# Attention: which engine copies which half of the transposed probabilities, and how the reciprocals of the row sums are spread

## The chip, the cores and the metric

The kernel runs on one core of a Trainium2 chip, in one launch. The metric is the device time of the launch in microseconds (us); lower is better. Engines: PE is TensorE (matmuls; PEld are its weight loads), DVE is VectorE, ACT is ScalarE, POOL is GpSimd, SP is SyncE, which issues most DMAs.

## The reference, cut to what matters

Two layers over x (2 x 512 x 1024) and a context (2 x 1024 x 1024): cross attention, a feed-forward block, a quantised product and a stream mixer. The change lies in the cross attention of the first layer:

```
query = q @ w_q.T; key = k @ w_k.T; value = v @ w_v.T     # 32 heads of 32; 8 groups of keys and values, 4 heads each
scores = einsum('bghnd,bgsd->bghns', query, key) / D_HEAD ** 0.5
scores = where(mask, scores, finfo.min)
attention = softmax(scores, axis=-1)
out = einsum('bghns,bgsd->bghnd', attention, value)
```

There are 2 x 8 = 16 pairs of batch and group; each has 512 queries (4 tiles of 128), 4 heads and 1024 keys (8 tiles of 128).

## The kernel before, in words

Stage a makes the queries, keys and values, stage b (line 452) is the attention, stages c, d and e are the rest. The stages follow one another; stage b ends with a barrier of all engines, and stage c starts after it, with some of its weights loaded early.

Stage b works in steps. One step is one tile of 128 queries of one head: 16 steps (`STEPS`) for a pair of batch and group, 256 steps in all. A loop body of 32 steps (two pairs, u = 0 and 1) stands first, 6 times in a hardware loop, and last. Each engine has its own list of instructions, written out by hand; semaphores order them. In step k (with j = k mod 16):

- TensorE (`body`, line 603) issues the scores of step k+2 (`score`, two matmuls of 512 keys into one of two PSUM buffers), then for the two halves f of the keys the four transposes of the probabilities `Pr` of step k into `psT` (line 621; the first half is called T1 below, the second T2), and between T1 and T2 the weighing of one tile of keys (`weigh`, line 575: four heads side by side, each 32 columns of the array, two records each). The weighing runs 8 steps behind: 8 steps (a unit: 4 heads x 2 query tiles) are collected in `PT`, and while the next 8 are transposed, one of 8 key tiles is weighed in each step.
- VectorE (`body`, line 729) masks the scores of step k+2 and takes their minimum (`mask_min`, line 700, one custom operation from PSUM to `Sc`), then copies the second half of the transposes of step k from `psT` to `PT` (`keep`, line 711).
- ScalarE (`body`, line 675) takes the exponential of step k+1 with the sum of each row (`exponentials`, line 647), then copies the first half of step k (`keep`, line 658).

What holds what: T1 and T2 of step k each wait until the copy of the same half of step k-1 is done, and T1 waits for the exponential of step k; the scores of step k+2 wait for the mask of step k; the mask waits for its scores; the exponential waits for its mask, and, with two `Pr` buffers, for T2 of two steps before.

The softmax is divided at the end. Each row is a query, but the output is held turned (head dimension by query), so the reciprocals of the 16 row sums of each query tile have to be spread over the partitions. For the pair that has just ended: VectorE takes the reciprocals (`reciprocals`, line 718, at j = 0), ScalarE copies the unscaled output (`keep_O`, line 669, j = 8), TensorE turns the reciprocals into 4 rows (`turn_rec`, line 590, j = 10, after T2), ScalarE copies these (`rec_rows`, line 665, j = 12), TensorE multiplies them by a constant 0/1 matrix `headsel` that gives each head its 32 partitions (`spread_rec`, line 599, j = 13, after T2), and VectorE multiplies (`normalise`, line 722, j = 15). SyncE stores the product and loads the next pair (line 546). GpSimd builds `ident` and `headsel` once.

Of the kernel before, what the change touches and what calls it, by code (L numbers as in the profile page):

```python
# [30 lines left out]
P = 128  # L31
# [420 lines left out]
def stage_b(nc, mask, QHd, QLd, KHd, KLd, Vd, AOd, early, start_early_loads):  # L452
# [4 lines left out]
    with ExitStack() as stack:  # L457
# [8 lines left out]
        UNIT = 2 * HPG  # L466
        UQ = 2 * P
        assert UNIT == NK
        ident = sb("b_ident", [P, P])
        headsel = sb("b_headsel", [HPG, P])  # L470
        mk8 = sb("b_mk8", [P, QT, S2], U8)
        mbias = sb("b_mbias", [P, QT, S2], BF16)
        Qs = sb("b_Qs", [P, 2, HPG, S], F32R)
        Ks = sb("b_Ks", [P, 2, S2], F32R)
        Vs = sb("b_Vs", [P, 2, NK, DH])
        Sc = sb("b_Sc", [P, 4, S2])
        Pr = sb("b_Pr", [P, 2, S2])
        PT = sb("b_PT", [P, 2, NK, HPG, UQ])
        mins = sb("b_mins", [P, 4])
        sums = sb("b_sums", [P, 2, STEPS])  # L480
        rec = sb("b_rec", [P, 2, STEPS])
        recT = sb("b_recT", [HPG, S])
        Os = sb("b_Os", [P, S])
        AOs = sb("b_AOs", [P, 2, S])
        psS = stack.enter_context(nc.psum_tensor("b_psS", [P, 2, S2], F32))
        psT = stack.enter_context(nc.psum_tensor("b_psT", [P, 2, NK // 2, P], F32))

        psO = stack.enter_context(nc.psum_tensor("b_psO", [P, 2, S], F32))

        setup = sem("b_setup")  # L490
        selready = sem("b_selready")
        mask_in = sem("b_mask_in")
        mbias_ready = sem("b_mbias")
        waited = sem("b_waited")
# [7 lines left out]
        kept = [sem(f"b_kept{f}") for f in range(2)]  # L502
        weighed = sem("b_weighed")
        rec_ready = sem("b_rec")
        rec_turned = sem("b_recturned")
        recT_ready = sem("b_recT")
        spread = sem("b_spread")
        O_kept = sem("b_Okept")
        AO_ready = sem("b_AO")
# [52 lines left out]
        @block.tensor  # L562
        def _(pe):
            def score(it, k, very_first=False):

                u, j = divmod(k, STEPS)
                qt, h = divmod(j, HPG)
                if j == 0 and not very_first:
                    pe.wait_ge(qkv_in[u], (it + 1) * (16 * QKV_DMAS))
                for n in range(2):  # L570
                    last = pe.matmul(psS[:, k % 2, n * HALF:(n + 1) * HALF], Qs[:, u, h, qt * P:(qt + 1) * P],  # L571
                                     Ks[:, u, n * HALF:(n + 1) * HALF], start=True, stop=True)
                last.then_inc(scored, 1)

            def weigh(it, k, first=False):

                u, unit, kt = (k // UNIT - 1) // 2 % 2, k // UNIT - 1, k % UNIT
                if kt == 0:
                    pe.wait_ge(kept[0], it * BODY + k)
                    pe.wait_ge(kept[1], it * BODY + k)  # L580
                    if unit % 2 == 0 and not first:
                        pe.wait_ge(AO_ready, it * 2 + (u - 1))
                cols = slice(unit % 2 * UQ, (unit % 2 + 1) * UQ)
                for h in range(HPG):
                    last = pe.matmul(psO[h * DH:(h + 1) * DH, u, cols], Vs[:, u, kt, :], PT[:, unit % 2, kt, h, :],  # L585
                                     start=(kt == 0), stop=(kt == NK - 1))
                if kt == NK - 1:
                    last.then_inc(weighed, 1)

            def turn_rec(bg, u):  # L590

                pe.wait_ge(rec_ready, bg + 1)
                pe.wait_ge(O_kept, bg + 1)
                for qt in range(QT):
                    last = pe.transpose(psO[0:HPG, u, qt * P:(qt + 1) * P], rec[:, u, qt * HPG:(qt + 1) * HPG],
                                        ident[:])
                last.then_inc(rec_turned, 1)

            def spread_rec(bg, u):
                pe.wait_ge(recT_ready, bg + 1)  # L600
                pe.matmul(psO[:, u, :], headsel[:], recT[:], start=True, stop=True).then_inc(spread, 1)

            def body(it, first=False, last=False):
                for k in range(BODY):
                    u, j = divmod(k, STEPS)

                    if not (last and k + 2 >= BODY):
                        pe.wait_ge(masked, it * BODY + (k + 1))
                        if k + 2 < BODY:
                            score(it, k + 2)  # L610
                        else:
                            score(it + 1, k + 2 - BODY)
                    pe.wait_ge(probs, it * BODY + (k + 1))
                    for f in range(2):
                        if f == 1 and not (first and k < UNIT):
                            weigh(it, k, first)
                        if not (first and k == 0):
                            pe.wait_ge(kept[f], it * BODY + k)
                        for t in range(NK // 2):
                            kt = f * (NK // 2) + t  # L620
                            last_t = pe.transpose(psT[:, f, t, :], Pr[:, k % 2, kt * P:(kt + 1) * P], ident[:])  # L621
                        last_t.then_inc(turned[f], 1)

                    if not (first and u == 0):
                        if j == UNIT + 2:
                            turn_rec(it * 2 + (u - 1), 1 - u)
                        if j == UNIT + 5:
                            spread_rec(it * 2 + (u - 1), 1 - u)

            pe.wait_ge(setup, 2)  # L630
            pe.wait_ge(selready, 4)
            pe.wait_ge(first_in, 16 * 8)
            score(0, 0, very_first=True)
            pe.wait_ge(qkv_in[0], 16 * QKV_DMAS)
            score(0, 1)
            body(0, first=True)
            with pe.Fori(1, BG // 2 - 1) as it:
                body(it)
            body(BG // 2 - 1, last=True)
            for k in range(UNIT):  # L640
                weigh(BG // 2, k)
            turn_rec(BG - 1, 1)
            spread_rec(BG - 1, 1)

        @block.scalar
        def _(act):
            def exponentials(it, k, first=False):

                act.wait_ge(masked, it * BODY + (k + 1))
                if not (first and k < 2):  # L650
                    act.wait_ge(turned[1], it * BODY + (k - 1))
                u, j = divmod(k, STEPS)
                if j == 0 and not first:
                    act.wait_ge(rec_ready, it * 2 + (u - 1))
                act.activation(Pr[:, k % 2, :], Sc[:, k % 4, :], ACT.Exp, bias=mins[:, k % 4:k % 4 + 1], scale=-1.0,  # L655
                               accum_out=sums[:, u, j:j + 1]).then_inc(probs, 1)

            def keep(it, k, first=False):
                act.wait_ge(turned[0], it * BODY + (k + 1))
                if not (first and k < 2 * UNIT):  # L660
                    if k % UNIT == 0:
                        act.wait_ge(weighed, it * (BODY // UNIT) + (k // UNIT - 1))
                act.copy(PT[:, (k // UNIT) % 2, 0:NK // 2, k % HPG, queries(k)], psT[:, 0, :, :]).then_inc(kept[0], 1)  # L663

            def rec_rows(bg, u):
                act.wait_ge(rec_turned, bg + 1)
                act.copy(recT[:], psO[0:HPG, u, :]).then_inc(recT_ready, 1)

            def keep_O(bg, u, first=False):
                act.wait_ge(weighed, (bg + 1) * (STEPS // UNIT))  # L670
# [4 lines left out]
            def body(it, first=False, last=False):  # L675
                for k in range(BODY):
# [6 lines left out]
                    if not (first and u == 0):  # L683
                        if j == UNIT:
                            keep_O(it * 2 + (u - 1), 1 - u, first and u == 1)
                        if j == UNIT + 4:
                            rec_rows(it * 2 + (u - 1), 1 - u)

            act.dma_start(mk8[:], mask.rearrange("(t p) k -> p t k", p=P)).then_inc(mask_in, 16)
            exponentials(0, 0, True)  # L690
# [2 lines left out]
                body(it)  # L693
            body(BG // 2 - 1, last=True)
            keep_O(BG - 1, 1)
            rec_rows(BG - 1, 1)

        @block.vector
        def _(dve):
# [9 lines left out]
                                         accum_out=mins[:, k % 4:k % 4 + 1]).then_inc(masked, 1)  # L709

            def keep(it, k, first=False):
                dve.wait_ge(turned[1], it * BODY + (k + 1))
                if not (first and k < 2 * UNIT):
                    if k % UNIT == 0:
                        dve.wait_ge(weighed, it * (BODY // UNIT) + (k // UNIT - 1))
                dve.tensor_copy(PT[:, (k // UNIT) % 2, NK // 2:NK, k % HPG, queries(k)], psT[:, 1, :, :]).then_inc(kept[1], 1)  # L716

            def reciprocals(bg, u):
                dve.wait_ge(probs, (bg + 1) * STEPS)
# [9 lines left out]
            def body(it, first=False, last=False):  # L729
                for k in range(BODY):  # L730
# [6 lines left out]
                    if not (first and u == 0):  # L737
                        if j == 0:
                            reciprocals(it * 2 + (u - 1), 1 - u)
                        if j == UNIT + 7:  # L740
                            normalise(it * 2 + (u - 1), 1 - u, None if first else it * 16)

            dve.sem_inc(stored[1], 16)
# [15 lines left out]
        @block.gpsimd  # L759
        def _(pool):  # L760
            identity(pool, ident, setup)
            pool.memset(headsel[:], 1.0).then_inc(selready, 1)
            pool.wait_ge(selready, 1)
            pool.affine_select(out=headsel[:], in_=headsel[:], compare_op=ALU.is_ge, fill=0.0, base=0,
                               pattern=[[1, P]], channel_multiplier=-DH).then_inc(selready, 1)
            pool.wait_ge(selready, 2)
            pool.affine_select(out=headsel[:], in_=headsel[:], compare_op=ALU.is_ge, fill=0.0, base=DH - 1,
                               pattern=[[-1, P]], channel_multiplier=DH).then_inc(selready, 2)

# [1233 lines left out]
```

## Time and profile before

| | us |
|---|---|
| median of 3 runs (lowest to highest) | 1259.8 (1259.29 to 1261.71) |
| profiled execution | 1259.68 |
| its span, first to last instruction | 1258.0 |
| PE, DVE, ACT busy over the span | 1068.5, 903.9, 666.7 |
| mean granted TensorE clock | 0.925 |

The profile shows one execution. The span is what the instructions cover; the rest up to the time of the execution lies around it. The granted clock is the share of full speed that TensorE was given (1.00 is 2.4 GHz, 0.50 is 1.2 GHz). A matmul's record shows when it starts and a modelled end; matmuls overlap, so differences between starts tell more than durations. In a timeline, instructions of one line that follow each other are merged (x4). The attention's steps run from about 241 to 792 us of the span.

### The profile page before, as it was taken

The numbers are of one execution on the slowest core, as the hardware profiler recorded it, in microseconds if no ns is written. First come the engines' busy times: TensorE is split into PE (matmuls) and PEld (weight loads), VectorE is DVE, ScalarE is ACT, GpSimd is POOL, SyncE is SP. The second block draws the span as 40 slices with busy tenths as digits, with TensorE's granted clock in tenths as the row PEclk, the third lists the DMA queues.
The fourth block names the chain that finished last, engine by engine and source line by source line (L and its number), as shares of the span: only waits on it lengthen the run. The fifth ranks groups of instructions, "written<-read, shape, count | busy, mean of one in ns | idle before, by whom it ended". The sixth has DMA issues, their size and how long they took to land. (4 is left out here: it accounts for less than half of the span.)

```text
span 1258.0 us, 20626 instructions
## 1 busy us (share of the span) xinstructions
PE 1068.5 (85%) x6955; PEld 748.6 (60%) x6960; DVE 903.9 (72%) x1889; ACT 666.7 (53%) x1142; POOL 126.5 (10%) x107
## 2 busy tenths in 40 slices
PE   4999999499999999999999999699999957623108
PEld 4788777366666666666666666467888823311007
DVE  7345741498888988888888888546633346689998
ACT  4223310388888888888888888412311155533214
POOL 3110200000000000000000000000112045134300
PEclk9999999699999999999999999899999989855559
DMA  4677931841122222222211221454130000000003
GB/s 185 238 268 257 391 107 57 227 150 36 42 55 63 63 63 63 63 58 63 52 43 35 62 64 43 175 192 140 52 134 0 1 1 0 12 1 0 0 1 134
DMA packets 55626, 112.86 MB, mean 90 GB/s; under 512 B 7788, under 2 KB 21228, under 8 KB 55452
## 3 DMA queue, kind: packets, MB, share of 16 engines
q1 hardware_dynamic: 54988, 111.73, 28.6%
q8 instruction: 27, 0.44, 0.1%
q10 hardware_dynamic: 528, 0.52, 0.1%
q14 instruction: 19, 0.16, 0.0%
q0 software_dynamic: 64, 0.00, 0.0%
HBM read 83.99 MB, written 27.26 MB: 88 GB/s over the span
## 5 line engine op out<-in xcount | busy, mean ns | idle before, releaser
L655 ACT ACTIVATE b_Pr<-b_Sc,b_mins 128x1024 f32<-128x1024 f32 x256 | 295.3, 1153 | 93.1 <-PE b_psT L621 70.1
L707 DVE CUSTOM_DVE_ANT_0 b_Sc<-b_psS,b_mbias 128x1024 f32<-128x1024 f32 x256 | 312.3, 1220 | 28.0 <-PE b_psS L571 27.9
L621 PE MATMUL b_psT<-b_ident,b_Pr 128*128 128x128 f32 x2048 | 321.7, 280 | 0.6
L621 PEld LDWEIGHTS b_psT<-b_ident,b_Pr 128*128 128x128 f32 x2048 | 235.4, 141 | 140.4 <-issue 97.6
L716 DVE COPY b_PT<-b_psT 128x512 f32<-128x512 f32 x256 | 176.9, 691 | 42.7 <-PE b_psT L621 40.1
L571 PE MATMUL b_psS<-b_Ks,b_Qs 128*128 128x512 f32 x512 | 183.3, 439 | 16.4 <-DMA b_Qs<-QLd 13.6
L585 PE MATMUL b_psO<-b_PT,b_Vs 128*32 128x256 f32 x2048 | 162.1, 390 | 1.3 <-DVE b_PT L716 0.9
L663 ACT COPY b_PT<-b_psT 128x512 f32<-128x512 f32 x256 | 145.5, 569 | 13.8 <-PE b_psT L621 13.2
L571 PEld LDWEIGHTS b_psS<-b_Ks,b_Qs 128*128 128x128 f32 x512 | 78.2, 193 | 28.5 <-issue 24.4
L270 PE MATMUL a_psM<-XTh,WTh 128*128 128x512 f32 x192 | 76.0, 396 | 3.6 <-DVE WTl L345 3.6
L270 PE MATMUL a_psM<-XTl,WTh 128*128 128x512 f32 x192 | 75.5, 393 | 0.0
L270 PE MATMUL a_psM<-XTh,WTl 128*128 128x512 f32 x192 | 75.4, 393 | 0.0
L585 PEld LDWEIGHTS b_psO<-b_PT,b_Vs 128*32 128x32 f32 x2048 | 42.0, 108 | 44.6 <-issue 43.8
L314 ACT ACTIVATE a_oh<-a_psM 128x512 fp32r<-128x512 f32 x24 | 14.4, 601 | 100.4 <-PE a_psM L270 98.0
L1637 PE MATMUL e_psT<-e_XN,e_dg 128*128 x128 | 29.9, 399 | 41.2 <-DVE XR L1892 41.2
L381 DVE SCALAR_TENSOR_TENSOR a_ol<-a_psM,a_oh 128x512 fp32r<-128x512 f32 x24 | 16.6, 691 | 66.2 <-ACT a_oh L314 66.2
L1053 ACT ACTIVATE c_sd<-c_mv,c_eps 128x1 f32<-128x1 f32 x16 | 4.8, 297 | 103.4 <-DVE c_mv L1140 103.4
L1133 DVE TENSOR_TENSOR XR<-XR,c_psM 128x1024 f32<-128x1024 f32 (+1 forms) x16 | 19.5, 1218 | 54.9 <-PE c_psM L959 54.9
L60 POOL MEMSET c_ident<- 128x128 f32 x1 | 0.2, 206 | 573.6 <-POOLq L457 573.6
L1637 PEld LDWEIGHTS e_psT<-e_XN,e_dg 128*128 128x128 f32 x128 | 25.7, 202 | 45.8 <-issue 41.9
L959 PE MATMUL c_psM<-WEh,c_Lh 128*128 128x512 f32 x128 | 50.5, 394 | 0.0
L1621 PE MATMUL e_psP<-e_ident,e_xp 128*128 128x128 f32 x16 | 5.5, 448 | 52.8 <-POOL e_xp L1927 52.8
(221 smaller groups left out, 1698.1 us busy)
## 6 DMA issues: line engine op xcount, KB each, us to landing
a_xn<-in_ctx_turned SPq DMA_DIRECT2D x16, 512.0 KB, 3.4
XS<-in_ctx SPq DMA_DIRECT2D x16, 512.0 KB, 5.8
b_Qs<-QHd SPq DMA_DIRECT2D x30, 256.0 KB, 4.6
b_Qs<-QLd SPq DMA_DIRECT2D x30, 256.0 KB, 5.4
XS<-in_x SPq DMA_DIRECT2D x8, 512.0 KB, 9.1
a_wst<-in_L_xattn_w_q SPq DMA_DIRECT2D x8, 512.0 KB, 5.0
Q2d<-a_q SPq DMA_DIRECT2D x16, 256.0 KB, 4.7
QHd<-a_oh SPq DMA_DIRECT2D x16, 256.0 KB, 4.1
```

The source lines that it names most:

```text
L270: last = pe.matmul(psM[:, slot, :], a[:, w_slot, k, :], m[:, k, cols], start=(k == 0 and a is WTh and m is mh), stop=(k == KT - 1 and a is ...
L381: dve.scalar_tensor_tensor(out=ol[:, slot, :], in0=psM[:, ps_slot, :], scalar=scale, in1=oh[:, slot, :].bitcast(F32), op0=ALU.mult, op1=AL ...
L571: last = pe.matmul(psS[:, k % 2, n * HALF:(n + 1) * HALF], Qs[:, u, h, qt * P:(qt + 1) * P], Ks[:, u, n * HALF:(n + 1) * HALF], start=True ...
L585: last = pe.matmul(psO[h * DH:(h + 1) * DH, u, cols], Vs[:, u, kt, :], PT[:, unit % 2, kt, h, :], start=(kt == 0), stop=(kt == NK - 1))
L621: last_t = pe.transpose(psT[:, f, t, :], Pr[:, k % 2, kt * P:(kt + 1) * P], ident[:])
L655: act.activation(Pr[:, k % 2, :], Sc[:, k % 4, :], ACT.Exp, bias=mins[:, k % 4:k % 4 + 1], scale=-1.0, accum_out=sums[:, u, j:j + 1]).then ...
L663: act.copy(PT[:, (k // UNIT) % 2, 0:NK // 2, k % HPG, queries(k)], psT[:, 0, :, :]).then_inc(kept[0], 1)
L707: dve.tensor_tensor_reduce(out=Sc[:, k % 4, :], in0=psS[:, k % 2, :], in1=mbias[:, qt, :], scale=1.0, scalar=3.4e38, op0=ALU.add, op1=ALU.min,
L716: dve.tensor_copy(PT[:, (k // UNIT) % 2, NK // 2:NK, k % HPG, queries(k)], psT[:, 1, :, :]).then_inc(kept[1], 1)
L959: last = pe.matmul(psM[:, u, cols], a[:, u, k, :], w[:, k, cols], start=(k == 0 and i == 0), stop=(k == KT - 1 and i == 2))
L1133: dve.tensor_tensor(row, row, psM[:, u, :], ALU.add).then_inc(added, 1)
L1637: last = pe.matmul(psX(u)[:, i * CH:(i + 1) * CH], dg[:, u, n, i, :], XN[:, ds(t, 1), n * CH:(n + 1) * CH].rearrange("p a n -> p (a n)"), ...
```

## The change

- VectorE copies the first half of the transposes (T1's) and ScalarE the second (T2's). The order of each engine's list is otherwise the same.
- `Pr` has four buffers instead of two.
- The turn of the reciprocals, ScalarE's copy of the rows and the matmul with `headsel` are gone. Instead, for each of 4 query tiles and 4 heads, one matmul has as its stationary operand one column of `rec`, repeated 32 times by a stride of zero, and as its moving operand the identity; it writes 32 partitions x 128 queries of `psO`. These 16 matmuls stand between T1 and the weighing at j = 11.
- `normalise` is at j = 13 instead of 15.
- `headsel` isn't built any more.

```diff
@@ -466,29 +466,28 @@
         UNIT = 2 * HPG
         UQ = 2 * P
         assert UNIT == NK
+        PR = 4
+        PARTS = (slice(0, NK // 2), slice(NK // 2, NK))
         ident = sb("b_ident", [P, P])
-        headsel = sb("b_headsel", [HPG, P])
         mk8 = sb("b_mk8", [P, QT, S2], U8)
         mbias = sb("b_mbias", [P, QT, S2], BF16)
         Qs = sb("b_Qs", [P, 2, HPG, S], F32R)
         Ks = sb("b_Ks", [P, 2, S2], F32R)
         Vs = sb("b_Vs", [P, 2, NK, DH])
         Sc = sb("b_Sc", [P, 4, S2])
-        Pr = sb("b_Pr", [P, 2, S2])
+        Pr = sb("b_Pr", [P, PR, S2])
         PT = sb("b_PT", [P, 2, NK, HPG, UQ])
         mins = sb("b_mins", [P, 4])
         sums = sb("b_sums", [P, 2, STEPS])
         rec = sb("b_rec", [P, 2, STEPS])
-        recT = sb("b_recT", [HPG, S])
         Os = sb("b_Os", [P, S])
         AOs = sb("b_AOs", [P, 2, S])
         psS = stack.enter_context(nc.psum_tensor("b_psS", [P, 2, S2], F32))
-        psT = stack.enter_context(nc.psum_tensor("b_psT", [P, 2, NK // 2, P], F32))
+        psT = stack.enter_context(nc.psum_tensor("b_psT", [P, NK, P], F32))
 
         psO = stack.enter_context(nc.psum_tensor("b_psO", [P, 2, S], F32))
 
         setup = sem("b_setup")
-        selready = sem("b_selready")
         mask_in = sem("b_mask_in")
         mbias_ready = sem("b_mbias")
         waited = sem("b_waited")
...
@@ -587,18 +584,16 @@
                 if kt == NK - 1:
                     last.then_inc(weighed, 1)
 
-            def turn_rec(bg, u):
+            def spread_rec(bg, u):
 
                 pe.wait_ge(rec_ready, bg + 1)
                 pe.wait_ge(O_kept, bg + 1)
                 for qt in range(QT):
-                    last = pe.transpose(psO[0:HPG, u, qt * P:(qt + 1) * P], rec[:, u, qt * HPG:(qt + 1) * HPG],
-                                        ident[:])
-                last.then_inc(rec_turned, 1)
-
-            def spread_rec(bg, u):
-                pe.wait_ge(recT_ready, bg + 1)
-                pe.matmul(psO[:, u, :], headsel[:], recT[:], start=True, stop=True).then_inc(spread, 1)
+                    for h in range(HPG):
+                        one = rec[:, u, qt * HPG + h:qt * HPG + h + 1].to_broadcast([P, DH])
+                        last = pe.matmul(psO[h * DH:(h + 1) * DH, u, qt * P:(qt + 1) * P], one, ident[:],
+                                         start=True, stop=True)
+                last.then_inc(spread, 1)
 
             def body(it, first=False, last=False):
                 for k in range(BODY):
@@ -616,19 +611,13 @@
                             weigh(it, k, first)
                         if not (first and k == 0):
                             pe.wait_ge(kept[f], it * BODY + k)
-                        for t in range(NK // 2):
-                            kt = f * (NK // 2) + t
-                            last_t = pe.transpose(psT[:, f, t, :], Pr[:, k % 2, kt * P:(kt + 1) * P], ident[:])
+                        for kt in range(NK)[PARTS[f]]:
+                            last_t = pe.transpose(psT[:, kt, :], Pr[:, k % PR, kt * P:(kt + 1) * P], ident[:])
                         last_t.then_inc(turned[f], 1)
-
-                    if not (first and u == 0):
-                        if j == UNIT + 2:
-                            turn_rec(it * 2 + (u - 1), 1 - u)
-                        if j == UNIT + 5:
+                        if f == 0 and j == UNIT + 3 and not (first and u == 0):
                             spread_rec(it * 2 + (u - 1), 1 - u)
 
             pe.wait_ge(setup, 2)
-            pe.wait_ge(selready, 4)
             pe.wait_ge(first_in, 16 * 8)
             score(0, 0, very_first=True)
             pe.wait_ge(qkv_in[0], 16 * QKV_DMAS)
...
@@ -647,24 +635,20 @@
             def exponentials(it, k, first=False):
 
                 act.wait_ge(masked, it * BODY + (k + 1))
-                if not (first and k < 2):
-                    act.wait_ge(turned[1], it * BODY + (k - 1))
+                if not (first and k < PR):
+                    act.wait_ge(turned[1], it * BODY + (k + 1 - PR))
                 u, j = divmod(k, STEPS)
                 if j == 0 and not first:
                     act.wait_ge(rec_ready, it * 2 + (u - 1))
-                act.activation(Pr[:, k % 2, :], Sc[:, k % 4, :], ACT.Exp, bias=mins[:, k % 4:k % 4 + 1], scale=-1.0,
+                act.activation(Pr[:, k % PR, :], Sc[:, k % 4, :], ACT.Exp, bias=mins[:, k % 4:k % 4 + 1], scale=-1.0,
                                accum_out=sums[:, u, j:j + 1]).then_inc(probs, 1)
 
             def keep(it, k, first=False):
-                act.wait_ge(turned[0], it * BODY + (k + 1))
+                act.wait_ge(turned[1], it * BODY + (k + 1))
                 if not (first and k < 2 * UNIT):
                     if k % UNIT == 0:
                         act.wait_ge(weighed, it * (BODY // UNIT) + (k // UNIT - 1))
-                act.copy(PT[:, (k // UNIT) % 2, 0:NK // 2, k % HPG, queries(k)], psT[:, 0, :, :]).then_inc(kept[0], 1)
-
-            def rec_rows(bg, u):
-                act.wait_ge(rec_turned, bg + 1)
-                act.copy(recT[:], psO[0:HPG, u, :]).then_inc(recT_ready, 1)
+                act.copy(PT[:, (k // UNIT) % 2, PARTS[1], k % HPG, queries(k)], psT[:, PARTS[1], :]).then_inc(kept[1], 1)
 
             def keep_O(bg, u, first=False):
                 act.wait_ge(weighed, (bg + 1) * (STEPS // UNIT))
...
@@ -709,11 +690,12 @@
                                          accum_out=mins[:, k % 4:k % 4 + 1]).then_inc(masked, 1)
 
             def keep(it, k, first=False):
-                dve.wait_ge(turned[1], it * BODY + (k + 1))
+                dve.wait_ge(turned[0], it * BODY + (k + 1))
                 if not (first and k < 2 * UNIT):
                     if k % UNIT == 0:
                         dve.wait_ge(weighed, it * (BODY // UNIT) + (k // UNIT - 1))
-                dve.tensor_copy(PT[:, (k // UNIT) % 2, NK // 2:NK, k % HPG, queries(k)], psT[:, 1, :, :]).then_inc(kept[1], 1)
+                dve.tensor_copy(PT[:, (k // UNIT) % 2, PARTS[0], k % HPG, queries(k)], psT[:, PARTS[0], :]
+                                ).then_inc(kept[0], 1)
 
             def reciprocals(bg, u):
                 dve.wait_ge(probs, (bg + 1) * STEPS)
@@ -737,7 +719,7 @@
                     if not (first and u == 0):
                         if j == 0:
                             reciprocals(it * 2 + (u - 1), 1 - u)
-                        if j == UNIT + 7:
+                        if j == UNIT + 5:
                             normalise(it * 2 + (u - 1), 1 - u, None if first else it * 16)
 
             dve.sem_inc(stored[1], 16)
...
```

## Rows read from the trace of the kernel before

**Rows 1.** windows; busy us of PE, PEld, DVE, ACT, POOL; granted clock, DMA share, GB/s

```profile
500.00:600.00 100.00, 99.92 (x847) 63.94 (x846) 87.97 (x145) 81.70 (x144) 0.00 (x0) 1.00 0.25 58
...
246.00:256.00 10.00, 9.48 (x61) 6.61 (x60) 10.00 (x17) 9.75 (x18) 0.00 (x0) 1.00 1.03 401
```

**Rows 2.** groups: 300 to 700 us, the page's; busy us, mean ns | idle

```profile
L655 ACT ACTIVATE b_Pr<-b_Sc,b_mins 128x1024 f32<-128x1024 f32 x185 | 213.4, 1153 | 61.9 <-PE b_psT L621 52.0 <-DVE b_mins L707 8.2
...
L571 PE MATMUL b_psS<-b_Ks,b_Qs 128*128 128x512 f32 x512 | 183.3, 439 | 16.4 <-DMA b_Qs<-QLd 13.6
```

**Rows 3.** timeline of one step: start us, us, engine line, out<-in, count [idle before]

```profile
506.11 0.71 PE L571 MATMUL b_psS<-b_Ks,b_Qs 128*128 128x512 f32 x2
506.66 0.60 PE L621 MATMUL b_psT<-b_ident,b_Pr 128*128 128x128 f32 x4
...
507.19 0.16 PEld L585 LDWEIGHTS b_psO<-b_PT,b_Vs 128*32 128x32 f32 x8 [0.17 <-issue]
507.19 0.64 PE L585 MATMUL b_psO<-b_PT,b_Vs 128*32 128x256 f32 x8
...
507.76 0.66 PE L621 MATMUL b_psT<-b_ident,b_Pr 128*128 128x128 f32 x4
...
508.17 0.71 PE L571 MATMUL b_psS<-b_Ks,b_Qs 128*128 128x512 f32 x2
...
508.45 0.69 DVE L716 COPY b_PT<-b_psT 128x512 f32<-128x512 f32 x1 [0.18 <-PE b_psT L621]
...
509.10 1.23 DVE L707 CUSTOM_DVE_ANT_0 b_Sc<-b_psS,b_mbias 128x1024 f32<-128x1024 f32 x1
```

**Rows 4.** timeline around the turn (j = 10) and the spread (j = 13)

```profile
503.20 0.66 PE L621 MATMUL b_psT<-b_ident,b_Pr 128*128 128x128 f32 x4
...
504.05 0.71 PE L571 MATMUL b_psS<-b_Ks,b_Qs 128*128 128x512 f32 x2
...
509.81 0.66 PE L621 MATMUL b_psT<-b_ident,b_Pr 128*128 128x128 f32 x4
...
511.45 0.73 PE L571 MATMUL b_psS<-b_Ks,b_Qs 128*128 128x512 f32 x2
```

**Rows 5.** timeline, ScalarE's copy of the output at j = 8, three groups apart

```profile
499.39 0.59 ACT L673 COPY b_Os<-b_psO 128x512 f32<-128x512 f32 x1
...
603.47 0.58 ACT L673 COPY b_Os<-b_psO 128x512 f32<-128x512 f32 x1
```

**Rows 6.** timeline of the first steps, without weighing

```profile
247.68 0.69 DVE L716 COPY b_PT<-b_psT 128x512 f32<-128x512 f32 x1
...
248.41 0.14 PEld L621 LDWEIGHTS b_psT<-b_ident,b_Pr 128*128 128x128 f32 x1 [0.23 <-DVE b_PT L716]
...
248.94 0.56 ACT L663 COPY b_PT<-b_psT 128x512 f32<-128x512 f32 x1
...
249.42 0.69 DVE L716 COPY b_PT<-b_psT 128x512 f32<-128x512 f32 x1
...
249.62 0.42 PEld L621 LDWEIGHTS b_psT<-b_ident,b_Pr 128*128 128x128 f32 x4 [0.52 <-ACT b_Pr L655]
...
250.02 1.21 DVE L707 CUSTOM_DVE_ANT_0 b_Sc<-b_psS,b_mbias 128x1024 f32<-128x1024 f32 x1
...
251.16 0.69 DVE L716 COPY b_PT<-b_psT 128x512 f32<-128x512 f32 x1
```

**Rows 7.** timeline, transposes whose first weights were not loaded ahead

```profile
789.06 0.66 PE L621 MATMUL b_psT<-b_ident,b_Pr 128*128 128x128 f32 x4
...
789.65 0.64 PE L585 MATMUL b_psO<-b_PT,b_Vs 128*32 128x256 f32 x8
```

**Rows 8.** timeline of the attention's end

```profile
793.31 3.21 PEld L585 LDWEIGHTS b_psO<-b_PT,b_Vs 128*32 128x32 f32 x64 [1.08 <-issue]
...
797.06 0.59 ACT L673 COPY b_Os<-b_psO 128x512 f32<-128x512 f32 x1 [5.12 <-PE b_psO L585]
...
800.21 0.69 DVE L727 TENSOR_TENSOR b_AOs<-b_psO,b_Os 128x512 f32<-128x512 f32 x1 [6.26 <-PE b_psO L601]
```

More of the change, by code:

```diff
@@ L504, in stage_b @@
         rec_ready = sem("b_rec")
-        rec_turned = sem("b_recturned")
-        recT_ready = sem("b_recT")
         spread = sem("b_spread")
@@ L641, in _ @@
                 weigh(BG // 2, k)
-            turn_rec(BG - 1, 1)
             spread_rec(BG - 1, 1)
@@ L685, in body @@
                             keep_O(it * 2 + (u - 1), 1 - u, first and u == 1)
-                        if j == UNIT + 4:
-                            rec_rows(it * 2 + (u - 1), 1 - u)
             act.dma_start(mk8[:], mask.rearrange("(t p) k -> p t k", p=P)).then_inc(mask_in, 16)
@@ L695, in _ @@
             keep_O(BG - 1, 1)
-            rec_rows(BG - 1, 1)
         @block.vector
@@ L761, in _ @@
             identity(pool, ident, setup)
[L762 to L768, printed above, removed]
 class EarlyLoads:
```

## Prediction

> **What bounds the kernel now.** I read the windows first, then the groups by line, then the timeline of one step, because the change lies in the attention alone. Of 256 steps (16 groups of 16), each does on TensorE: the scores of step n+2 (two matmuls), the first four transposes of step n (T1), eight records of the weighing (the product with V), the last four transposes (T2). From 300 to 700 us TensorE is busy 99.9% of the time at the full granted clock, VectorE 88%, ScalarE 82% [rows 1]. Busy matmul time does not prove a bound, so the gaps decide. ScalarE's exponentials idle 61.9 us in 185 steps, 52.0 of it for TensorE's transposes [rows 2]; VectorE's copy idles 0.18 us for T2 [rows 3]; TensorE's own starts follow each other without a named wait: scores 506.11, T1 506.66, weighing 507.19, T2 507.76, scores 508.17 [rows 3], that is 0.55 + 0.53 + 0.57 + 0.41 = 2.06 us. So TensorE's stream is the bound of a plain step, and the others have little slack.
>
> A group of 16 steps takes (603.47 - 499.39) / 3 = 34.69 us [rows 5]. Sixteen plain steps are 32.9, so 1.8 us per group is the reciprocals' way. Its two parts show: T2 to scores is 503.20 to 504.05 = 0.85 with the turn of the reciprocals, 0.44 over the plain 0.41; with the spread it is 509.81 to 511.45 = 1.64, 1.23 over it [rows 4]. Together 1.67; the last 0.1 or so is smaller waits.
>
> **The spread.** Removed per group: those 1.8 us on TensorE, and ScalarE's row copy. Added: 16 fp32 matmuls, 32 columns stationary and 128 moving, in the gap between T1 and the weighing. They have the weighing's tile shape, so the change of shape that already stands between T1 and the weighing is made once, not twice. The price: 64 weight-load records (8 key tiles) of the closing weighing take 3.21 us, less the last tile's 0.16, so 3.05 / 7 = 0.436 us for four heads of 256 moving columns [rows 8, 3]. Four query tiles of 128 columns are half of that each, 4 x 0.218 = 0.87 us, if the columns set it; if the records set it, 4 x 0.436 = 1.74. Matmuls of this shape run four side by side, and eight weight loads end within 0.16 us [rows 3], so I take 0.87 and keep 1.74 for the range. Gain: (1.81 - 0.87) x 15 groups inside the loop = 14.1 us. After the last group the way from the copy of the output to the last product is 797.06 to 800.21 = 3.15 us [rows 8]; without the turn and the row copy it is about that copy and one spread with their hand-overs, 0.59 + 0.87 + 0.4 = 1.9: gain 1.3.
>
> The Trainium skill speaks against this term. TensorE: Matmul & The Clock Gate, section "Wait — 56ns, not 53.3ns?", says that starts on TensorE never come closer than about 25 ns however few columns are streamed. By that rule 64 records (32 loads, 32 matmuls) would cost 1.6 us, and the gain would be some 3 us instead of 14. Rows 3 do not bear it out for this shape: eight loads with a mean of 108 ns each are over 0.16 us after the first starts, under 8 ns apart.
>
> **The swap of the copies.** VectorE now copies the first half (made by T1), ScalarE the second (by T2). Both engines' copies stay what they cost; what moves is which copy gates T1. T1 of step n writes the first half of PSUM again, so it waits for the first copy of step n-1. VectorE's queue is unchanged: mask n+1, copy n-1, mask n+2, copy n. So that copy stands behind mask n+1, which waits for the scores n+1, which TensorE issues only in step n-1, just ahead of T1 of n-1. This is a loop over two steps, with each link a difference of starts:
> - scores to mask: 508.17 to 509.10 = 0.93 [rows 3]. The mask follows the copy at 508.45 by 0.65 there, and by 0.60 where nothing holds it (249.42 to 250.02 [rows 6]), so it waits for its scores even now, and 0.93 is that wait's length.
> - mask to the copy behind it, if nothing else holds it: 250.02 to 251.16 = 1.14 [rows 6], from the first eight steps, where there is no weighing and VectorE alone sets a period of 249.42 to 251.16 = 1.74.
> - VectorE's copy to transposes that wait for it: 247.68 to the weight load at 248.41, which the profile puts down to that copy, 0.73, and 0.01 to the matmul: 0.74 [rows 6].
> - T1 to the next scores: 0.53 + 0.57 + 0.41 = 1.51 where the first weights are loaded ahead. A T1 that was held has not got them: 789.06 to 789.65 = 0.59 to the weighing instead of 0.53 [rows 7]. So 1.57.
>
> The loop is 0.93 + 1.14 + 0.74 + 1.57 = 4.38 us for two steps, 2.19 a step against 2.055. TensorE can't stay at 2.055: from scores n+1 to T1 of step n it has 2.06 + 0.55 = 2.61 us, and the copy gives it 0.93 + 1.14 + 0.74 = 2.81. Price: 0.135 us in each step that has both a weighing and scores, 256 - 8 - 2 = 246 of them: +33.2 us. The first steps without weighing: the same links with 0.92 from T1 to scores, 3.73 / 2 = 1.865 against 1.74, some 7 steps, +0.9.
>
> Bounds of the loop: below, a copy that hands over at its end (0.69) and a T1 with weights loaded, 0.93 + 1.14 + 0.69 + 1.51 = 4.27, 2.135 a step, +20 us. Above, ScalarE's hand-over (copy at 248.94 and 0.56 long, weight load at 249.62, 0.12 after its end [rows 6]) on VectorE's copy, 0.84, and the mask's whole 1.23 instead of 1.14: 4.57, 2.285 a step, +57. I take the rows of the same operation, 4.38.
>
> In the kernel before the same test holds with slack: T2 waited for VectorE's copy, and T2 comes 1.65 after the scores of its step instead of 0.55, which is 1.10 us more room.
>
> **Four buffers for the exponentials.** They take away ScalarE's wait for T2 [rows 2]. ScalarE was not the bound: its exponential and copy fill about 1.15 + 0.56 of a step [rows 2, 6]; now it is held by the mask instead. A mask is 1.23 long [rows 3], so an exponential of 1.15 can end some 3.4 us after its scores, and T1 wants it a whole two steps after them, 4.9. Worth nothing, at most a shield. ScalarE's second copy is gated by T2 and wanted by the next T2, one period later, with about a microsecond of room; it costs nothing unless ScalarE gets behind by that.
>
> **The rest.** The product with the spread reciprocals comes two steps earlier. It is 0.6 us of VectorE between a copy and the next mask; the loop leaves VectorE about 0.45 idle there, so I count nothing and keep 0.2 x 15 = 3 us above. Its store goes out earlier, ahead of nothing that SyncE's queue needs. The column mask that GpSimd no longer builds was hidden: the first scores waited 13.6 us for a load [rows 2]; without that cover it would be worth under 1.5 us.
>
> **Sum** on the profiled execution's 1259.68 us (span 1258.0; the median of the runs is 1259.8, so the two agree): + 33.2 + 0.9 - 14.1 - 1.3 = + 18.7, 1278.4 us. The stages behind start after the attention ends and get the whole difference.
>
> **Rivals.**
> - T1's new gate doesn't bite, and only the cheaper spread is left: 1259.7 - 15.4 = 1244. For it: VectorE's row of idle time, and that 0.2 us is all by which the gate is late (2.81 against 2.61), so the links would have to be 0.2 us shorter together. Against: each link is a measured difference of starts in this trace. 13%. This is the side of faster.
> - The gate bites harder, at 2.285 or more a step: + 57 + 1 - 15 = 1303. For it: the hand-over of 0.12 after ScalarE's copy, on the very transposes that are concerned. 10%.
> - The spread costs by records, 1.74 us a group, with the loop as forecast: 0.87 x 16 = 14 us more, 1292. It's the skill's rule above as a mechanism here: by that rule's own figure it would be 1290. The closing weighing's 16 records in 0.436 us, 27 ns a record, could be read either way. 15%.
> - The gate bites, but at the low bound of 2.135: + 20 + 1 - 15 = 1265. 12%.
> - The forecast itself, 1269 to 1287: 50%.
>
> A measurement of this kernel tells about 0.2% (2.5 us) from no change. Faster by more 0.14 (the first rival and the last hundredth of the low loop), within it 0.05 (a low loop that the spread just pays), slower 0.81. Range 1262 to 1303: it leaves out the first rival and the top of the second.
>
> **What would show it.** In the profile after: weight loads of T1 that wait for VectorE's copy in every second step, where before there were few; scores to T1 0.55 in one step and about 0.8 in the next; steps that average 2.19; masks that idle for scores; exponentials that idle for the mask and no longer for T2; T1 to weighing near 1.4 in the step with the spread; still the full granted clock, as in the first eight steps, where TensorE also pauses [rows 1]. It is wrong if scores to T1 stays 0.55 in every step (first rival), if the spread step is over 1 us longer than its neighbours (third), or if TensorE's waits name ScalarE.

## The result and the profile after

The changed kernel takes 1287.94 us (median of 4 runs, 1287.45 to 1288.95) against 1260.76 before (4 runs, 1259.29 to 1262.26) beside it: ratio 1.0217, 95% interval 1.0199 to 1.0234. It is 27 us slower. The forecast was 1278.4, in a range of 1262 to 1303. The span grew from 1258.0 to 1285.6 us, 27.6.

The windows view of the changed kernel (columns as in [rows 1]):

```profile
500.00:600.00 100.00, 96.87 (x884) 58.17 (x885) 82.12 (x137) 76.69 (x135) 0.00 (x0) 1.00 0.17 41
```

No engine is as full as it was: TensorE fell from 99.92 to 96.87, VectorE from 87.97 to 82.12, ScalarE from 81.70 to 76.69. The clock is full, as before. A kernel that gets slower while its engines get emptier has a new wait somewhere. The groups of 300 to 700 us say where each engine stands still (busy us, mean ns | idle before it):

```profile
L688 DVE CUSTOM_DVE_ANT_0 b_Sc<-b_psS,b_mbias 128x1024 f32<-128x1024 f32 x175 | 214.3, 1225 | 70.2 <-PE b_psS L568 69.7
L643 ACT ACTIVATE b_Pr<-b_Sc,b_mins 128x1024 f32<-128x1024 f32 x175 | 201.7, 1153 | 0.0
L615 PEld LDWEIGHTS b_psT<-b_ident,b_Pr 128*128 128x128 f32 x1402 | 148.3, 140 | 137.8 <-issue 136.0
...
L697 DVE COPY b_PT<-b_psT 128x512 f32<-128x512 f32 x176 | 120.7, 686 | 0.0
...
L651 ACT COPY b_PT<-b_psT 128x512 f32<-128x512 f32 x176 | 103.1, 586 | 92.9 <-PE b_psT L615 91.7
```

Where ScalarE's exponentials idled for the transposes [rows 2], its copies do now, 0.53 us each. VectorE's copies never wait any more; its masks wait 0.4 us each for scores. What TensorE waits for is not named here: of the 137.8 us in which its weight loads for the transposes stand still, 136.0 are put down to "issue". The starts have to show it. Two steps in the timeline of the changed kernel, some lines left out:

```profile
500.90 0.71 PE L568 MATMUL b_psS<-b_Ks,b_Qs 128*128 128x512 f32 x2
...
500.91 0.69 DVE L697 COPY b_PT<-b_psT 128x512 f32<-128x512 f32 x1
...
501.71 0.42 PEld L615 LDWEIGHTS b_psT<-b_ident,b_Pr 128*128 128x128 f32 x4 [0.54 <-issue]
501.74 0.63 PE L615 MATMUL b_psT<-b_ident,b_Pr 128*128 128x128 f32 x4
...
502.30 0.64 PE L582 MATMUL b_psO<-b_PT,b_Vs 128*32 128x256 f32 x8
...
502.87 0.66 PE L615 MATMUL b_psT<-b_ident,b_Pr 128*128 128x128 f32 x4
...
503.28 0.71 PE L568 MATMUL b_psS<-b_Ks,b_Qs 128*128 128x512 f32 x2
...
503.83 0.61 PE L615 MATMUL b_psT<-b_ident,b_Pr 128*128 128x128 f32 x4
504.05 1.15 ACT L643 ACTIVATE b_Pr<-b_Sc,b_mins 128x1024 f32<-128x1024 f32 x1
504.21 1.22 DVE L688 CUSTOM_DVE_ANT_0 b_Sc<-b_psS,b_mbias 128x1024 f32<-128x1024 f32 x1 [0.55 <-PE b_psS L568]
...
505.35 0.71 PE L568 MATMUL b_psS<-b_Ks,b_Qs 128*128 128x512 f32 x2
505.37 0.08 DVE L688 DVE_READ_ACCUMULATOR2_ANT b_mins<- 128x1 f32 x1
505.37 0.69 DVE L697 COPY b_PT<-b_psT 128x512 f32<-128x512 f32 x1
...
506.20 0.63 PE L615 MATMUL b_psT<-b_ident,b_Pr 128*128 128x128 f32 x4
```

Scores to T1 is 0.84 in one step (500.90 to 501.74), 0.55 in the next (503.28 to 503.83), 0.85 again (505.35 to 506.20), where it was 0.55 in plain steps before [rows 3]. From 300 to 700 us long and short follow each other without an exception, 87 of 175 distances long. The circle can be read off: T1 501.74, scores 503.28 (1.54), mask 504.21 (0.93), copy 505.37 (1.16), T1 506.20 (0.83). That is 4.46 us for two steps, 2.23 a step against 2.055.

Two things could hold T1: the exponential of its step and the copy of the step before. The exponential of 504.05 is 1.15 long and done, with the reading of its row sum, 0.9 before T1 at 506.20; the copy is done 0.15 before it. The trace also keeps TensorE's record of its wait for that copy, a semaphore instruction of 0.05 us on line 613:

```profile
L613 PEldq EVENT_SEMAPHORE  x255: 51/51/51, 244.7 to 820.5; - x128
```

In all 176 steps from 300 to 700 us this record starts 0.04 after VectorE's copy ends, and in 165 of them the first weight load of T1 follows it by 0.08. So the copy is what T1's first weight load waits for.

The way of the reciprocals, once in 16 steps, in the changed kernel's TensorE timeline:

```profile
519.54 0.63 PE L615 MATMUL b_psT<-b_ident,b_Pr 128*128 128x128 f32 x4
520.10 1.08 PE L594 MATMUL b_psO<-b_ident,b_rec 128*32 128x128 f32 x32
521.00 0.61 PE L582 MATMUL b_psO<-b_PT,b_Vs 128*32 128x256 f32 x8
```

From the spread to the weighing is 0.90 us, all it costs; it was 0.44 + 1.23 in two places [rows 4], over the plain distances. The group of 16 steps, by ScalarE's copy of the output as in [rows 5]:

```profile
515.08 0.59 ACT L657 COPY b_Os<-b_psO 128x512 f32<-128x512 f32 x1
...
624.70 0.59 ACT L657 COPY b_Os<-b_psO 128x512 f32<-128x512 f32 x1
```

(624.70 - 515.08) / 3 = 36.54 us against 34.69, 1.85 more. It is made of 8 circles of 4.46, 35.7, and one spread, 0.9. The first and the fifteenth of these copies, in the kernel before and in the changed one:

```profile
291.00 0.59 ACT L673 COPY b_Os<-b_psO 128x512 f32<-128x512 f32 x1
...
777.00 0.59 ACT L673 COPY b_Os<-b_psO 128x512 f32<-128x512 f32 x1
```

```profile
296.17 0.59 ACT L657 COPY b_Os<-b_psO 128x512 f32<-128x512 f32 x1
...
807.22 0.59 ACT L657 COPY b_Os<-b_psO 128x512 f32<-128x512 f32 x1
```

Between them lie 486.00 and 511.05 us, 25.05 more. The first copy is already 5.17 late, and what comes after the fifteenth is 1.6 shorter. So the attention ends 28.7 us later (its last product starts at 828.87 instead of 800.21); the span grew by 27.6, and where the stages behind made up the last 1.1 is not shown.

### The profile page after: what moved, and what is told of

The parts are those of the page before. It is cut to its first block and busy times, and to the rows that moved or that the text cites. A ratio compares the mean times of both kernels' runs of the same rounds, so it can differ in the third digit from the quotient of the medians.

```text
span 1285.6 us, 21435 instructions
## 1 busy us (share of the span) xinstructions
PE 1074.1 (84%) x7371; PEld 731.0 (57%) x7376; DVE 896.6 (70%) x1889; ACT 659.0 (51%) x1126; POOL 126.7 (10%) x104
## 5 line engine op out<-in xcount | busy, mean ns | idle before, releaser
L615 PE MATMUL b_psT<-b_ident,b_Pr 128*128 128x128 f32 x2048 | 325.4, 282 | 20.0 <-DVE b_PT L697 7.2
L615 PEld LDWEIGHTS b_psT<-b_ident,b_Pr 128*128 128x128 f32 x2048 | 218.0, 141 | 200.2 <-issue 193.5
L651 ACT COPY b_PT<-b_psT 128x512 f32<-128x512 f32 x256 | 150.0, 586 | 132.6 <-PE b_psT L615 131.2
L934 PE MATMUL c_psM<-WEh,c_Ll 128*128 128x512 f32 x128 | 49.9, 390 | 0.0
```

The costliest lines, as they stand in the source:

```text
L615: last_t = pe.transpose(psT[:, kt, :], Pr[:, k % PR, kt * P:(kt + 1) * P], ident[:])
L651: act.copy(PT[:, (k // UNIT) % 2, PARTS[1], k % HPG, queries(k)], psT[:, PARTS[1], :]).then_inc(kept[1], 1)
L934: last = pe.matmul(psM[:, u, cols], a[:, u, k, :], w[:, k, cols], start=(k == 0 and i == 0), stop=(k == KT - 1 and i == 2))
```

## The experiments

The diffs below are shortened. The theory: the swap puts T1 into a circle through VectorE's queue (scores, mask, copy, T1, scores), which costs 0.17 us a step, while the spread by itself gains some 15 us. Rivals: the new spread or the buffers hold TensorE; ScalarE's late second copy does; VectorE is too busy. All with 3 timed rounds, 4 runs each, against runs of the kernel before on the same chip: median 1259.96 for e1 to e4, 1260.81 for e5 to e7 (7 runs each).

**e1, the copies put back** in the changed kernel:

```diff
-act.wait_ge(turned[1], ...); act.copy(PT[..., PARTS[1], ...], psT[:, PARTS[1], :]).then_inc(kept[1], 1)
+act.wait_ge(turned[0], ...); act.copy(PT[..., PARTS[0], ...], psT[:, PARTS[0], :]).then_inc(kept[0], 1)
-dve.wait_ge(turned[0], ...); dve.tensor_copy(PT[..., PARTS[0], ...], psT[:, PARTS[0], :]).then_inc(kept[0], 1)
+dve.wait_ge(turned[1], ...); dve.tensor_copy(PT[..., PARTS[1], ...], psT[:, PARTS[1], :]).then_inc(kept[1], 1)
```

> The changed kernel with only the two copies put back: ScalarE copies T1's half, VectorE T2's. The new spread and four buffers stay. Loop theory (T1 of step n waits for VectorE's copy of step n-1, which stands behind mask n+1): the alternation of scores to T1 (0.55, 0.84) goes, all steps return to 2.055 us, and what is left is the spread at 0.90 instead of 1.81 per group: 15 x 0.91 + 1.3 = 15 us under before, 1245 us (1243 to 1248). Rival A, the new spread or the buffers hold TensorE: stays above 1260. Rival B, ScalarE's late second copy is what holds the steps: also 1245 here, told apart by e3.

Measured: 1246.45 us, ratio 0.9895 (0.9876 to 0.9914). TensorE's timeline of e1:

```profile
503.32 0.70 PE L568 MATMUL b_psS<-b_Ks,b_Qs 128*128 128x512 f32 x2
503.87 0.60 PE L615 MATMUL b_psT<-b_ident,b_Pr 128*128 128x128 f32 x4
504.40 0.64 PE L582 MATMUL b_psO<-b_PT,b_Vs 128*32 128x256 f32 x8
504.97 0.66 PE L615 MATMUL b_psT<-b_ident,b_Pr 128*128 128x128 f32 x4
505.38 0.71 PE L568 MATMUL b_psS<-b_Ks,b_Qs 128*128 128x512 f32 x2
505.92 0.60 PE L615 MATMUL b_psT<-b_ident,b_Pr 128*128 128x128 f32 x4
```

Scores to T1 is 0.55 in both steps and the step 2.06. So the swap carries all of the loss and more: 1288 to 1246. Rival A, that the new spread or the buffers hold TensorE, is out.

**e2, the swap alone**, in the kernel before, with four buffers and the old turn and spread:

```diff
-Pr = sb("b_Pr", [P, 2, S2])
+Pr = sb("b_Pr", [P, 4, S2])
-act.wait_ge(turned[0], ...)   # and psT[:, 0], kept[0]
+act.wait_ge(turned[1], ...)   # and psT[:, 1], kept[1]
-dve.wait_ge(turned[1], ...)   # and psT[:, 1], kept[1]
+dve.wait_ge(turned[0], ...)   # and psT[:, 0], kept[0]
```

> The kernel before with the copies swapped and four buffers for the exponentials, but with the old turn and spread of the reciprocals. Loop theory: 0.17 us in each of 246 steps and 1 us in the first ones, less up to 0.3 per group where the turn or the spread falls on a step that would have waited anyway: +38 to +43 us on before, 1299 to 1304. If the loss in the changed kernel came from the new spread instead: 1260.

Measured: 1297.08 us, ratio 1.0302 (1.0283 to 1.0321), 2 us under the expected band. Its group of 16 steps takes (628.58 - 517.45) / 3 = 37.04 us by the same copy, +2.35 on before; eight circles and the old 1.81 would be 37.5, so nearly 0.5 of the turn and spread falls into steps that would have waited, more than the 0.3 I allowed. The swap's loss (37 us) and the spread's gain (14, from e1) make 23; the changed kernel lost 27. The two don't simply add, because e2 hides waits under the turn and spread (0.45 x 15 = 7 us by the sum of the circles) and the changed kernel hides next to none (36.54 against 36.6); the size fits only roughly.

**e3, VectorE's copy ahead of its mask**, all else as in the changed kernel:

```diff
+                    keep(it, k, first)
                     if k + 2 < BODY:
                         mask_min(it, k + 2, first)
                     elif not last:
                         mask_min(it + 1, k + 2 - BODY)
-                    keep(it, k, first)
```

> The changed kernel with one line of VectorE's list moved: the copy of step k stands ahead of the mask of step k+2 instead of behind it. ScalarE still copies the second half. Loop theory: the copy no longer stands behind a mask that waits for scores; it starts 0.7 us after T1, the loop is cut, steps return to 2.055: 1245 us (1243 to 1249). Rival B, ScalarE's late second copy or the contention of the two engines at PSUM: nothing it does is changed, so 1288. Rival C, VectorE is simply too busy with a mask and a copy: 1288 too.

Measured: 1249.26 us, ratio 0.9918 (0.9896 to 0.9939), just above the expected band. The same instructions, the same engines for the same halves, and 38 us (ratio 1.0217 to 0.9918) go by the place of one copy in a queue. From its timeline:

```profile
503.45 0.60 PE L615 MATMUL b_psT<-b_ident,b_Pr 128*128 128x128 f32 x4
...
504.08 0.69 DVE L697 COPY b_PT<-b_psT 128x512 f32<-128x512 f32 x1 [1.10 <-PE b_psT L615]
...
504.69 1.22 DVE L688 CUSTOM_DVE_ANT_0 b_Sc<-b_psS,b_mbias 128x1024 f32<-128x1024 f32 x1
...
505.50 0.60 PE L615 MATMUL b_psT<-b_ident,b_Pr 128*128 128x128 f32 x4
```

The copy starts 0.63 after its T1 and is done 0.73 before the next T1 (504.77 to 505.50). Rivals B and C are out: ScalarE's second copy is as late as in the changed kernel (it starts 0.69 after T2 in both), and VectorE does the same work. Its groups of 16 steps are as long as those of e1, (632.34 - 530.61) / 3 = 33.91 and (629.58 - 527.82) / 3 = 33.92; the 2.8 us over e1 lie before the second group. Some 1.5 of them are in the first eight steps, where two steps of e3 take 3.86 us, 1.93 each, against 1.74 [rows 6]; the rest is open.

**e4, two buffers for the exponentials** in the changed kernel:

```diff
-        PR = 4
+        PR = 2
```

> The changed kernel with two buffers for the exponentials instead of four. ScalarE's copy of step k waits for T2 of step k and stands right ahead of the exponential k+2, so the buffer's wait for the same T2 is always met: no difference, 1288 within 1 us. If the four buffers carry something: over 2 us slower.

Measured: 1288.79 us, ratio 1.0231 (1.0214 to 1.0248), against 1.0217 (1.0199 to 1.0234) for the changed kernel. No difference: the four buffers carry nothing here.

**e5, a shorter copy in the circle.** VectorE copies three of its four tiles; the fourth is set to zero once, at the start, so that a part of the output is not computed:

```diff
-dve.tensor_copy(PT[..., PARTS[0], ...], psT[:, PARTS[0], :])
+dve.tensor_copy(PT[..., 0:3, ...], psT[:, 0:3, :])
```

> The changed kernel with VectorE's copy cut to three of its four tiles (the fourth tile of the weighed probabilities is left at zero, so a part of the output is not computed). The copy is a link of the loop, and 384 columns instead of 512 should take about 0.13 us less (a copy of 1024 columns takes 1.22, one of 512 0.69). Loop theory: 4.45 becomes 4.32 us for two steps, 0.066 a step over 246 steps: 16 us under the changed kernel, 1272 (1270 to 1274). If VectorE's copy is in no loop, its idle time for the scores only grows and nothing moves: 1288. If VectorE's whole work were the bound: 0.13 in each of 254 steps, 1254.

Measured: 1270.20 us, ratio 1.0081 (1.0059 to 1.0102). From its VectorE timeline:

```profile
500.17 1.23 DVE L688 CUSTOM_DVE_ANT_0 b_Sc<-b_psS,b_mbias 128x1024 f32<-128x1024 f32 x1 [0.55 <-PE b_psS L568]
...
501.31 0.55 DVE L697 COPY b_PT<-b_psT 128x384 f32<-128x384 f32 x1
...
504.48 1.22 DVE L688 CUSTOM_DVE_ANT_0 b_Sc<-b_psS,b_mbias 128x1024 f32<-128x1024 f32 x1 [0.54 <-PE b_psS L568]
```

The copy is 0.14 shorter, two steps are 4.31 instead of 4.46, and the kernel is 18 us faster. VectorE had idled for scores already: outside a circle a shorter copy would only have lengthened that idle time (1288), and if VectorE's whole work were the bound it would have given 1254. Taking work off an engine with idle time helped, one for one, though only in every second step.

**e6, the spread alone**: e1 with two buffers.

```diff
-        PR = 4
+        PR = 2
```

> The kernel with the copies put back and also the two buffers for the exponentials: of the change only the new spread (and the product two steps earlier) is left. The exponentials wait for T2 again, as before the change, but TensorE sets the step: same as with four buffers, 1246.5 within 1.5 us. If the buffers shield anything, over 2 us slower than that.

Measured: 1246.78 us, ratio 0.9893 (0.9872 to 0.9914), as e1. Of the whole change only the spread is worth keeping.

**e7, fewer changes of tile shape**, on e1:

```diff
-                        if f == 1 and not (first and k < UNIT):
+                        if f == 1 and not (first and k < UNIT) and k % 2 == 1:
+                            weigh(it, k - 1, first)
                             weigh(it, k, first)
```

> The copies put back, the new spread, and the weighing of two key tiles together in every odd step, none in the even ones. TensorE then changes between whole transposes and four narrow tiles once in two steps: T1 to weighing 0.53 and weighing to T2 0.57 hold about 0.10 + 0.14 over the 0.43 of the columns, so up to 0.24 per two steps. Against it: in the even steps T2 follows the T2 before by 1.39, less than VectorE's copy needs (0.69 + 0.84), which gives back 0.14. Net 0.10 per two steps, 12 us under the version with the copies back: 1234 (1228 to 1240). If the change of tile shape costs nothing: 1246 or more.

Measured: 1230.79 us, ratio 0.9765 (0.9744 to 0.9786), 30 us under before and the fastest here. TensorE's timeline of e7:

```profile
507.92 0.71 PE L568 MATMUL b_psS<-b_Ks,b_Qs 128*128 128x512 f32 x2
508.47 1.13 PE L616 MATMUL b_psT<-b_ident,b_Pr 128*128 128x128 f32 x8
509.36 0.72 PE L568 MATMUL b_psS<-b_Ks,b_Qs 128*128 128x512 f32 x2
509.91 0.60 PE L616 MATMUL b_psT<-b_ident,b_Pr 128*128 128x128 f32 x4
510.44 1.07 PE L582 MATMUL b_psO<-b_PT,b_Vs 128*32 128x256 f32 x16
511.44 0.66 PE L616 MATMUL b_psT<-b_ident,b_Pr 128*128 128x128 f32 x4
511.86 0.47 PE L568 MATMUL b_psS<-b_Ks,b_Qs 128*128 128x512 f32 x1
```

Two plain steps take 3.94 us (507.92 to 511.86) instead of 4.11. Two weighings end in T2 after 1.00, where one took 0.57, so the second costs 0.43, its columns. Of the 0.24 that were to be had, the expected 0.14 of giving back is only some 0.05: from T1 to the next scores it is 0.89, so T1 to T2 is 0.89 - 0.41 = 0.48 for 0.43 of columns. That would make 0.17 a pair, but the whole group of 16 steps is (619.90 - 521.38) / 3 = 32.84 us by ScalarE's copy of the output, 1.08 less than e1's 33.92, 0.135 a pair: one pair in a group is some 0.5 longer than the plain ones, in e1 it is 0.14. So the kernel came out 3 us better than expected, and not 9.

## Why the prediction was right

By its steps:

- **TensorE's stream is the bound, with little slack.** Right. In e1 and e3, without the circle, steps are 2.06 us again, and e7, which shortens TensorE's stream, is 16 us faster than e1.
- **The circle by the swapped copies.** Right in every sign and link, mis-sized in one. Scores to mask was taken at 0.93 and is 0.93; mask to copy 1.14, is 1.16; T1 to scores, held, 1.57, is 1.54; VectorE's copy to T1 was taken at 0.74 and is 0.83. Sum 4.38, measured 4.46. The 0.74 came from the row of a T2 that waited for VectorE's copy [rows 6]; T1 behaves as the other bound, worked out from ScalarE's hand-over at the same T1, 0.84. The nearer row was the one of the same place in TensorE's queue, not the one of the same engine that releases. The trace shows what lies in that place: T1 has the wait for the exponential ahead of that for the copy, and its wait for the copy is the separate record of line 613, 0.04 after the copy's end; the weight load follows 0.08 later, 0.12 after the end in all. T2 has one wait and no such record, and its weight load at 248.41 [rows 6] came 0.05 after the copy's end. ScalarE's copy in the kernel before was followed at T1 by the same record. That this record is the whole of the difference was not tried by a run. In price: (4.46 - 4.38) / 2 = 0.04 x 246 = 10 us, against the 9 us by which the forecast was too low.
- **Every second step waits.** Right: 0.84, 0.55, 0.85. The sign was to be weight loads of T1 that wait for VectorE's copy by name; from 300 to 700 us the profile names it ahead of 22 matmuls, 3.9 us in all, and puts 136.0 us of idle time before the weight loads down to "issue"; by this sign the circle would have been missed.
- **The first eight steps** were put at 3.73 for two. Scores at 251.62 and 255.35 are 3.73 apart, but by luck: two errors cancel in it. The hand-over is 0.83 again instead of 0.74 (copy 253.70, T1 254.53), and T1 to scores is 0.82 instead of 0.92 (254.53 to 255.35).
- **The spread by its columns, 0.87.** Measured 0.90. The gain was put at 15.4 us with the end; e1 gives 13.5 with an interval of 11 to 16. What was removed is less than the 1.81 of a group. Only 1.67 of it are the turn and the spread; the rest was taken for smaller waits, and a group of e1 still has 0.14 of those, 33.92 against 16 x 2.055 + 0.90 = 33.78.
- **The rule that spoke against it** was read too widely. The Trainium skill (TensorE: Matmul & The Clock Gate, section "Wait — 56ns, not 53.3ns?") gives its floor of about 25 ns from the start of one matmul to the start of the next, not for weight loads. By it the 32 matmuls of a spread would take 0.8 us, an estimate from the page's figure, under the 0.87 of the columns: it was no argument for 1.6. Nor does the floor hold here: the 32 matmuls start in fours, 7 ns apart within a four, one four some 109 ns after the other. The first four in the changed kernel, all started within 0.02 us, as each is 0.30 long:

```profile
520.10 0.32 PE L594 MATMUL b_psO<-b_ident,b_rec 128*32 128x128 f32 x4
```

- **After the last group**, 1.3 us: it is 827.01 to 828.87, 1.86 instead of 3.15. Right.
- **Four buffers cost and bring nothing.** Right by e4 and e6, but not for the reason given. The exponentials were to be held by the mask; they idle 0.0 us. ScalarE is held one instruction earlier, by its copy that waits for T2 (91.7 us), and the exponential follows that copy at once.
- **ScalarE has room.** Right by e3. **The product two steps earlier costs nothing**: e1's group holds it and all other small waits within 0.14.
- **The rivals.** The gate that doesn't bite would have been 1244; e1, in which T1 waits for ScalarE's copy as before, is at 1246. The harder gate (2.285) had the right hand-over but a mask of 1.23 that did not come; the truth, 2.23, lies between it and the forecast. The time alone would not have decided: 1287.94 is just above the 1269 to 1287 that were called the forecast itself, and 4 us under the 1292 of a spread that costs by its records. The spread's 0.90 rules that one out, and e1 does.

## What to carry to other kernels

Before work is moved from one engine to another, ask whose queue it will stand in, and ahead of it which wait. A copy that frees a single PSUM buffer belongs first in its engine's list, ahead of anything that waits for the engine that needs the buffer. A circle is found by adding differences of starts along it and comparing with the steps it spans; when all engines get emptier and the time longer, look for one, also where the profile names no engine as the cause of the wait. In this kernel, work that needs another tile shape of TensorE was cheapest next to work of that shape.

## What the runs showed of the hardware

- 32 weight loads and 32 matmuls of 32 stationary and 128 moving columns, fp32, in four column tiles take 0.90 us together, against 0.87 worked out from the weighing by columns alone: loading weights costs next to nothing beside the columns, and a stationary operand that is one column repeated by a stride of zero is hardly slower for it.
- A wait of TensorE that has another wait ahead of it (T1) stands in the trace as a record of 0.05 us, and the weight load comes 0.12 us after the end of the copy it waits for; where the wait is the only one (T2), it came after 0.05.
- Going from whole transposes to four narrow tiles costs TensorE about 0.10 us over the columns (0.53 for 0.43), and back 0.14 (0.57 for 0.43); e7 took away half of these changes and gained 16 us. What in the change costs the time is not shown.
- TensorE's granted clock was 1.00 from 300 to 400 and from 500 to 600 us in the changed kernel and in e2, though it paused in every second step, as in e1, e3 and e7, where it hardly did.
